# Down projection of a mixture-of-experts kernel in pairs of experts, with the array split into two row halves for what is left

## The chip, the cores and the metric

The kernel runs as one program on one core of a Trainium2 chip. The number that counts is the device time in microseconds (us), median of three runs: 970.37 us for the kernel before (966.24 to 972.15).

## The reference, cut to what matters

One layer: a linear attention with decay over 4096 tokens of width 512, a layer norm, a mixture of experts, a second layer norm. The change is in the experts. Each of 64 experts takes up to 128 tokens, has a hidden width of I = 192 and gives back rows of width 512:

```python
gx = xp[buf_tok]                                   # 64 x 128 x 512
gu = jnp.einsum('ech,ehi->eci', gx, gate_up_proj)  # 512 -> 2 * 192
g, u = jnp.split(gu, 2, axis=-1)
hid = jax.nn.silu(g) * u
eo = jnp.einsum('eci,eih->ech', hid, down_proj) * buf_w[..., None]   # 192 -> 512
routed = jnp.zeros((T + 1, h), x.dtype).at[buf_tok.reshape(-1)].add(eo.reshape(-1, h))[:T]
shared = jax.nn.silu(xf @ shared_gate_w.T) * (xf @ shared_up_w.T) @ shared_down_w.T
return (routed + shared).reshape(b, s, h)
```

All is float32. The reduction of the down projection (`eo`) runs over 192 rows, one and a half times the 128 rows of the TensorE array. The shared expert has a hidden width of 384 and sees all tokens.

## The kernel before

**Stages.** The kernel is written engine by engine, each with its own order written out by hand and semaphores between them. First come 32 attention steps (8 blocks of 512 tokens, 4 chunks each) with routing behind them, then the loop over 64 experts, then a tail that finishes the shared expert and the last layer norm.

**An expert on TensorE (PE).** For expert e the loop issues 12 products of `wgu_hi`, `wgu_lo` with `xgt_hi`, `xgt_lo` into one of `gu_ps` (gate and up), then `turn_rows(e + 1)` (4 transposes of the gathered rows `xg`), then `down(e - 1)`, then the shared units that `fills_of[e]` gives to this expert, then 2 transposes of `hid_e` into `ht_ps`. `down(e)` multiplies the turned hidden rows `hid_et` (two chunks of `IH` = 96 rows) with `wdn` into the one bank `eo_ps`. Both operands are plain float32, and the trace shows each such matmul as two instructions. `down(e)` waits for ScalarE's copy `hid_et` and for ScalarE's emptying of the bank (`eo_done`).

**The other engines.** ScalarE (ACT) copies: `tanh_e`, `xgt_hi` (`split_rows`), `wgu_hi` (`split_expert`), `eo` (`scale_rows`, one of NEO = 3 slots, which waits until the scatter of three experts before has landed, semaphores `rows_added`), then `hid_et`. It works these strictly in that order. GpSimd (POOL) issues `add_rows(e - 2)`, an indirect DMA that adds the 128 rows of `eo` into `acc_rows` in device memory, and `gather(e + 4)`, the rows for an expert four ahead. A scatter waits for the scatter two before it (`rows_added[e % 2]`). SyncE (SP) issues the loads: `wgu` (4 buffers, issued when the product that used the buffer is done) and `wdn` (3 buffers).

**Shared units.** The shared expert is cut into 64 units, 8 for a block of 512 tokens: six products (gate and up of three chunks, 12 matmuls each) and two pairs of output tiles (18 matmuls each). A unit writes one of three banks `proj_ps` (a pair of tiles two), by the rule take % 3, and waits for what emptied the bank three takes before. 8 units run among the last attention steps, 5 ahead of the experts, 21 among the experts, 30 behind them. For the last four blocks (`EARLY` = 4) an output tile is emptied out of its bank by VectorE (DVE) in `add_shared` (`fin_added`), which needs the finished sums of that block in `fin` and `odd`, loaded from `acc_rows`; SP issues these loads only after all 64 scatters have landed:

```python
sp.wait_ge(eo_done, NE)
sp.wait_ge(rows_added[0], 16 * NE // 2)
sp.wait_ge(rows_added[1], 16 * NE // 2)
for m in range(NFA):
    load_first(m)
```

Of the kernel before, what the change touches and what calls it, by code (L numbers as in the profile page):

```python
# [15 lines left out]
P = 128  # L16
# [29 lines left out]
def build(nc, x, x_t, w_qkv, w_out, decay_param, gate_t, w_gu, w_down, sg_t, su_t, sd_t, out):  # L46
# [10 lines left out]
    IH = I // 2  # L57
# [5 lines left out]
    NG, ND, NXG, AHEAD = 4, 3, 6, 4  # L63
    STEPS = NB * KC
    UNITS = 2 * SC + NJ // 2

    assert SC < NJ and KC == NJ and SI == GU and NB % 2 == 0
# [22 lines left out]
    wdn_buf = [both.place(f"wdn{i}", [IH, 2, D]) for i in range(2)]  # L90
# [91 lines left out]
    shared_stage = Map(nc, both.at - 2 * 4 * (KC * GU + 2 * D), both.at)  # L182
# [10 lines left out]
    wdn_buf += [late.place(f"wdn{i}", [IH, 2, D]) for i in range(2, ND)]  # L193
    assert late.at <= projected_end + 8 * 4 * BT

# [11 lines left out]
    hid_et = [late.place(f"hid_et{i}", [IH, 2, P]) for i in range(2)]  # L207
# [7 lines left out]
    fin_map = Map(nc, both.at - 2 * 4 * (KC * GU + 2 * D), both.at)  # L215
# [54 lines left out]
    HEAD = 2  # L270
# [42 lines left out]
    with ExitStack() as ctx:  # L313
# [10 lines left out]
        xg_ps, gu_ps, ht_ps, eo_ps = banks[3], banks[4:6], banks[6], banks[7]  # L324
# [74 lines left out]

        def x1_slot(i):  # L400
            return (NSTAGE + i) % NJ
# [4 lines left out]
        def _(sp):  # L406
# [38 lines left out]
            def load_down(e):  # L445
                if e >= ND:
                    sp.wait_ge(eo_mm, e - ND + 1)
                sp.dma_start(wdn_buf[e % ND][:, :, :], w_down[e]).then_inc(dn_in[e % ND], 16)
# [95 lines left out]
            for e in range(2, ND):  # L544
                load_down(e)
# [16 lines left out]
            for e in range(2):  # L562
                load_down(e)
# [14 lines left out]
            for e in range(NE):  # L578
                if e + NG < NE:
                    load_gate_up(e + NG)  # L580
                if e and e - 1 + ND < NE:
                    load_down(e - 1 + ND)
# [41 lines left out]
        def _(act):  # L624
# [112 lines left out]
            def unit():  # L737
                b, part = divmod(unit_at[0], UNITS)
                unit_at[0] += 1
                if part < 2 * SC:  # L740
                    c = part // 2
                    n = SC * b + c
                    if part % 2 == 0:
                        act.wait_ge(g_mm, n + 1)
                        if n:
                            act.wait_ge(silu_done, n)
                        ps = proj_ps[(unit_take(b) + part) % 3]
# [12 lines left out]
                for j in (2 * pair, 2 * pair + 1) if b < EARLY else ():  # L760
                    act.wait_ge(down_mm, NJ * b + j + 1)
                    if b == 0 and j == 0:
                        act.wait_ge(heads_mm, 2 * NB)
                    if b == 1 and j == 0:
                        act.wait_ge(rest_mm, NT)
                        act.wait_ge(out_mm, NT)
                        act.wait_ge(table_done, TABLE_JOINED)
                    if b >= len(shared_rows) and j == 0:
                        act.wait_ge(shared_out[b - len(shared_rows)], 16)
                    act.copy(shared_rows[b % len(shared_rows)][:, j, :], proj_ps[rows_take[b, j] % 3][:, :]).then_inc(rows_copied, 1)  # L770
# [104 lines left out]
            def scale_rows(e):  # L875
                act.wait_ge(eo_mm, e + 1)
                if e >= NEO:
                    act.wait_ge(rows_added[e % 2], 16 * ((e - NEO) // 2 + 1))
                act.activation(eo[eo_slot[e]][:, :], eo_ps[:, :], ACT.Copy, scale=xg[e % NXG][:, D + e:D + e + 1]).then_inc(eo_done, 1)  # L879
# [19 lines left out]
            for e in range(NE):  # L899
# [8 lines left out]
                if e:  # L908
                    scale_rows(e - 1)
# [5 lines left out]
                act.copy(hid_et[e % 2][:, :, :], ht_ps[0:IH, 0:2 * P].rearrange("p (h s) -> p h s", h=2)).then_inc(hid_et_done, 1)  # L915
# [40 lines left out]
        def _(dve):  # L956
# [232 lines left out]
            def finish_pair(n):  # L1189

                joined = [join_sums(n), join_sums(n + 1)]
                for t in range(2):
                    b, j = fin_order[n + t]
                    dve.wait_ge(down_mm, NJ * b + j + 1)
                    add_shared(n + t, proj_ps[rows_take[b, j] % 3][:, :], joined[t])
# [6 lines left out]
            def unit():  # L1202
                b, part = divmod(unit_at[0], UNITS)
                unit_at[0] += 1
                if part < 2 * SC:
                    c = part // 2
                    n = SC * b + c
                    ps = proj_ps[(unit_take(b) + part) % 3]
# [228 lines left out]
        def _(pool):  # L1437
# [167 lines left out]
        def _(pe):  # L1605
# [5 lines left out]
            def project(s, it, c, n, done):  # L1611
# [3 lines left out]
                if take >= 3:  # L1615
                    pe.wait_ge(*freed[take - 3])
                for k in range(KC):
# [4 lines left out]
                    mm = chain(proj_ps[take % 3][:, :], three(wqkv_hi[:, i, k, :], wqkv_lo[:, i, k, :], x_hi[it % 2][:, k, :],  # L1622
# [112 lines left out]
            def unit():  # L1735
                b, part = divmod(unit_at[0], UNITS)
                unit_at[0] += 1
                if part < 2 * SC:
# [6 lines left out]
                    pe.wait_ge(*freed[take - 3])  # L1745
# [3 lines left out]
                    chain(proj_ps[take % 3][:, :], products).then_inc(u_mm if part % 2 else g_mm, 1)  # L1749
# [3 lines left out]
                for late_chunk in (False, True):  # L1753
                    for j in pair:
# [3 lines left out]
                        if not late_chunk:  # L1758
                            pe.wait_ge(*freed[take - 3])
# [4 lines left out]
                        mm = chain(proj_ps[take % 3][:, :], products, first=not late_chunk, final=late_chunk)  # L1764
# [100 lines left out]
            for e in range(NE):  # L1865
# [10 lines left out]
                if e:  # L1876
                    down(e - 1)
                for _ in range(fills_of[e]):
# [4 lines left out]
                for k in range(2):  # L1883
                    mm = pe.transpose(ht_ps[0:IH, k * P:(k + 1) * P], hid_e[e % 2][:, k * IH:(k + 1) * IH], ident[:, :])
                mm.then_inc(ht_mm, 1)
            down(NE - 1)

# [33 lines left out]
```

## Time and profile before

| what | value |
|---|---|
| median of three runs | 970.37 us (966.24 to 972.15) |
| span of the profiled execution | 967.4 us |
| PE busy | 943.6 us, 98% |
| DVE, ACT, POOL busy | 683.8, 502.8, 466.4 us |
| last 40 us of the expert loop and start of the tail (840 to 880 us) | DMA at 214 GB/s |

The profile gives the execution it shows by its span, from the first to the last instruction; it has no other time for it. The span lies inside the range of the three runs, 3.0 us (0.3%) under their median. The stages in that span: attention to about 410 us, a mixed stretch to about 500 us, the experts to about 863 us, the tail to the end. PE busy is the time in which a matmul record is open, and records overlap, so 98% says that PE has almost always something in hand, not that it is at its peak.

### The profile page before, as it was taken

What the parts mean: (1) busy time and instruction counts of PE and PEld (TensorE: products, weight loads), DVE (VectorE), ACT (ScalarE), POOL (GpSimd) and SP (SyncE); (2) the same over time, 40 slices, a digit from 0 to 9 for tenths busy, and PEclk for the clock granted to TensorE, in tenths of its full rate; (3) what the DMA queues carried; (4) which work ended last, traced back from release to release, by engine and by line L of the source; (5) the groups of instructions that cost most, each with busy time, mean ns of one, the idle gap of its engine ahead of it and who ended that gap; (6) DMA issues with size and microseconds to landing.
All of it is one profiled execution on the core that took longest, in us unless ns stands there. A gap on an engine that the chain in (4) does not pass through costs nothing. (4 is left out here: it accounts for less than half of the span.)

```text
span 967.4 us, 15236 instructions
## 1 busy us (share of the span) xinstructions
PE 943.6 (98%) x4658; PEld 757.0 (78%) x4658; DVE 683.8 (71%) x1251; ACT 502.8 (52%) x1015; POOL 466.4 (48%) x543
## 2 busy tenths in 40 slices
PE   8999999999999999999999999999999999999996
PEld 7888888888888888877887777777767777777875
DVE  7977786969778796887766565566565665636776
ACT  5532434434443443534447665566655665635775
POOL 4002264565556554587234544445545454432564
PEclk9999999999999999989999999999999999999999
DMA  6343452444252434346569999999999999979973
GB/s 202 96 145 109 144 125 91 131 114 132 80 167 91 119 109 140 103 152 231 171 195 272 292 323 307 310 318 294 327 319 316 308 318 298 320 135 372 373 268 118
DMA packets 114191, 203.93 MB, mean 211 GB/s; under 512 B 18496, under 2 KB 56384, under 8 KB 113088
## 3 DMA queue, kind: packets, MB, share of 16 engines
q1 hardware_dynamic: 93584, 159.87, 50.6%
q0 software_dynamic: 19520, 35.75, 16.3%
q10 hardware_dynamic: 1008, 7.34, 2.0%
q8 instruction: 39, 0.64, 0.3%
q14 instruction: 40, 0.33, 0.1%
HBM read 143.03 MB, written 59.88 MB: 210 GB/s over the span
## 5 line engine op out<-in xcount | busy, mean ns | idle before, releaser
L1511 POOL DMA_INDIRECT slot_table<-tokens,slot_of x162 | 179.2, 1106 | 112.0 <-issue 59.6
L1553 POOL DMA_INDIRECT acc_rows<-eo,table_sb x64 | 112.0, 1750 | 170.4 <-ACT eo L879 133.0
L1608 PE MATMUL bank<-x_hi,wqkv_hi 128*128 128x512 f32 x384 | 153.2, 399 | 1.4 <-DVE wqkv_lo L963 1.3
L1376 DVE TENSOR_TENSOR wgu_lo<-wgu,wgu_hi 128x1536 fp32r<-128x1536 f32 x64 | 112.4, 1758 | 55.0 <-ACT wgu_hi L873 55.0
L1608 PE MATMUL bank<-x_hi,wqkv_lo 128*128 128x512 f32 x384 | 150.8, 393 | 0.0
L1608 PE MATMUL bank<-x_lo,wqkv_hi 128*128 128x512 f32 x384 | 150.6, 392 | 0.0
L1608 PE MATMUL bank<-wdn,hid_et 96*128 96x512 f32 x256 | 122.1, 599 | 7.6 <-ACT hid_et L915 7.6
L873 ACT CAST wgu_hi<-wgu 128x1536 fp32r<-128x1536 f32 x64 | 94.5, 1477 | 12.5 <-DMA wgu<-w_gu 12.1
L1542 POOL DMA_INDIRECT xg<-x_rows,table_sb x64 | 74.9, 1170 | 42.0 <-DVE table_sb L1111 22.7
L1608 PE MATMUL bank<-wgu_hi,xgt_hi 128*128 128x384 f32 x256 | 91.6, 358 | 0.0
L647 ACT ACTIVATE e<-bank 128x512 f32<-128x512 f32 x64 | 38.0, 594 | 97.3 <-PE bank L1608 97.3
L1608 PE MATMUL bank<-wgu_hi,xgt_lo 128*128 128x384 f32 x256 | 86.0, 336 | 0.0
L1608 PE MATMUL bank<-wgu_lo,xgt_hi 128*128 128x384 f32 x256 | 85.9, 336 | 0.0
L1608 PEld LDWEIGHTS bank<-x_hi,wqkv_hi 128*128 128x128 f32 x384 | 72.7, 189 | 16.3 <-DVE wqkv_lo L963 2.0
L1608 PEld LDWEIGHTS bank<-x_hi,wqkv_lo 128*128 128x128 f32 x384 | 72.5, 189 | 16.0
L1608 PEld LDWEIGHTS bank<-x_lo,wqkv_hi 128*128 128x128 f32 x384 | 72.6, 189 | 14.8
L1608 PEld LDWEIGHTS bank<-wdn,hid_et 96*128 96x128 f32 x256 | 43.5, 190 | 40.2 <-issue 30.7
L1403 DVE SCALAR_TENSOR_TENSOR silu_e<-tanh_e,bank 128x192 f32<-128x192 f32 x64 | 22.6, 353 | 66.9 <-ACT tanh_e L903 66.7
L1495 POOL TENSOR_SCALAR rstd<-mv 128x1 f32<-128x1 f32 x32 | 9.2, 286 | 115.3 <-DVE mv L990 114.0
L879 ACT ACTIVATE eo<-bank,xg 128x512 f32<-128x512 f32 x64 | 44.3, 692 | 39.2 <-DMA acc_rows<-eo,table_sb 33.9
L1608 PE MATMUL bank<-wout_hi,att_hi 128*128 128x512 f32 x128 | 52.0, 407 | 1.7 <-issue 1.2
L903 ACT ACTIVATE tanh_e<-bank 128x192 f32<-128x192 f32 x64 | 21.2, 331 | 61.6 <-PE bank L1608 61.3
(179 smaller groups left out, 2211.6 us busy)
## 6 DMA issues: line engine op xcount, KB each, us to landing
wgu<-w_gu SPq DMA_DIRECT2D x64, 768.0 KB, 8.8
wdn<-w_down SPq DMA_DIRECT2D x64, 384.0 KB, 8.8
xres<-x SPq DMA_DIRECT2D x32, 256.0 KB, 3.2
x_turned<-x1t SPq DMA_DIRECT2D x32, 256.0 KB, 2.8
x_rows<-x SPq DMA_DIRECT2D x32, 256.0 KB, 3.1
acc_rows<-x SPq DMA_DIRECT2D x32, 256.0 KB, 3.1
fin<-acc_rows SPq DMA_DIRECT2D x8, 1024.0 KB, 12.1
odd<-acc_rows SPq DMA_DIRECT2D x8, 1024.0 KB, 13.5
```

The source lines that it names most:

```text
L647: act.activation(e_sb[q][:, :], ps[:, :], ACT.Exp)
L873: act.copy(wgu_hi[e % 2][:, :, :], wgu_buf[e % NG][:, :, :]).then_inc(wgu_hi_done, 1)
L879: act.activation(eo[eo_slot[e]][:, :], eo_ps[:, :], ACT.Copy, scale=xg[e % NXG][:, D + e:D + e + 1]).then_inc(eo_done, 1)
L903: act.activation(tanh_e[:, :], gu_ps[e % 2][:, 0:I], ACT.Tanh, scale=0.5).then_inc(tanh_e_done, 1)
L1376: dve.tensor_tensor(wgu_lo[e % NG][:, :, :], wgu_buf[e % NG][:, :, :], wgu_hi[e % 2][:, :, :].bitcast(F32), ALU.subtract).then_inc(wgu_lo_ ...
L1403: dve.scalar_tensor_tensor(out=silu_e[:, :], in0=tanh_e[:, :], scalar=1.0, in1=ps[:, 0:I], op0=ALU.add, op1=ALU.mult).then_inc(silu_e_done, 1)
L1495: pool.tensor_scalar(rstd[i][:, :], mv[i][:, 1:2], EPS_NORM, None, ALU.add).then_inc(norm_done, 1)
L1511: pool.indirect_dma_start(table_dram, bass.IndirectOffsetOnAxis(slot_of[:, i, k:k + 1], 0), tokens[:, i:i + 1], None, bounds_check=SLOTS - ...
L1542: pool.indirect_dma_start(xg[e % NXG][:, :], None, x1_dram, bass.IndirectOffsetOnAxis(table_sb[:, e:e + 1], 0), bounds_check=T - 1, oob_is ...
L1553: pool.indirect_dma_start(acc_dram[e % 2], bass.IndirectOffsetOnAxis(table_sb[:, e:e + 1], 0), eo[eo_slot[e]][:, :], None, bounds_check=T ...
L1608: mm = pe.matmul(out_ap, a, b, start=first and i == 0, stop=final and i == len(products) - 1)
```

## The change

`down` no longer takes 192 rows as 96 + 96. For a pair of experts (even e and odd e) the weights come as one tile of three planes of 128 rows: 128 rows of the even expert, 128 rows of the odd one, and a plane that holds the 64 rows left of the even expert in rows 0 to 63 and the 64 left of the odd one in rows 64 to 127. `down(e)` is now one matmul over 128 rows; behind the odd one, `down_rest(p)` issues four matmuls of 64 rows and 256 columns, alternately in the upper and the lower row half, into two banks. Bank 2 is lent by the shared units for this while the expert loop lasts (they use banks 0 and 1 then). ScalarE scales both experts of a pair behind each other, in the iteration after the pair. `HEAD` goes from 2 to 6, so that 25 shared units (21 before) run among the experts and 26 (30 before) behind them, and units stand at odd experts alone. The weight loads are half as many and twice as large, with 2 buffers of a pair instead of 3 of an expert.

```diff
-    NG, ND, NXG, AHEAD = 4, 3, 6, 4
+    NG, ND, NXG, AHEAD = 4, 2, 6, 4
...
-    hid_et = [late.place(f"hid_et{i}", [IH, 2, P]) for i in range(2)]
+    hid_et = [late.place(f"hid_et{i}", [P, 2, P]) for i in range(2)]
...
-    HEAD = 2
+    HEAD = 6
...
-        while done < total and (done - first_units) * NE < (e + 1) * (total - first_units):
+        while e % 2 and done < total and (done - first_units) * NE < (e + 1) * (total - first_units):
...
-        xg_ps, gu_ps, ht_ps, eo_ps = banks[3], banks[4:6], banks[6], banks[7]
+        xg_ps, gu_ps, ht_ps, eo_ps = banks[3], banks[4:6], banks[6], [banks[7], banks[2]]
...
+        for take in range(3 * STEPS, len(freed)):
+            lent = first_units <= unit_of(take) < total
+            if lent and not eo_lent:
+                eo_emptied, eo_lent = freed[last_in[2]], True
+            bank = min((0, 1) if lent else (0, 1, 2), key=lambda n: last_in[n])
+            bank_of.append(bank)
+            if bank == 2 and eo_lent:
+                emptied.append((eo_done, NE))
+                eo_lent = False
...
+            def load_down(p):
+                if p >= ND:
+                    sp.wait_ge(eo_mm, 2 * (p - ND + 1))
+                sp.dma_start(wdn_buf[p % ND][:, :, :], w_down[p]).then_inc(dn_in[p % ND], 16)
...
-                if e:
+                if e and e % 2 == 0:
+                    scale_rows(e - 2)
                     scale_rows(e - 1)
...
-            for e in range(NE):
-                if e >= 2:
-                    add_rows(e - 2)
-                if e + AHEAD < NE:
-                    gather(e + AHEAD)
+            for e in range(0, NE, 2):
+                for n in (e, e + 1):
+                    if e:
+                        add_rows(n - 2)
+                    if n + AHEAD < NE:
+                        gather(n + AHEAD)
...
             def down(e):
+                p, r = divmod(e, 2)
                 pe.wait_ge(hid_et_done, e + 1)
-                pe.wait_ge(dn_in[e % ND], 16 * (e // ND + 1))
-                if e:
-                    pe.wait_ge(eo_done, e)
-                chain(eo_ps[:, :], [(hid_et[e % 2][:, k, :], wdn_buf[e % ND][:, k, :]) for k in range(2)]).then_inc(eo_mm, 1)
+                pe.wait_ge(dn_in[p % ND], 16 * (p // ND + 1))
+                if p:
+                    pe.wait_ge(eo_done, e - 1)
+                elif r:
+                    pe.wait_ge(*eo_emptied)
+                pe.matmul(eo_ps[r][:, :], hid_et[r][:, 1 - r, :], wdn_buf[p % ND][:, r, :], start=True, stop=False)
+
+            def down_rest(p):
+
+                for half in range(2):
+                    cols = slice(half * D // 2, (half + 1) * D // 2)
+                    for r in range(2):
+                        rows = slice(r * REM, (r + 1) * REM)
+                        mm = pe.matmul(eo_ps[r][:, cols], hid_et[r][rows, r, :], wdn_buf[p % ND][rows, 2, cols], start=False, stop=half == 1)
+                        if half:
+                            mm.then_inc(eo_mm, 1)
```

The order of PE in the middle of the loop, before: two experts without a shared unit between them, the products `wgu` left out.

```order
L1844 MATMUL bank3<-ident_49,xg3_184 128x128 [waits xgt_lo_done,xg_in3]
L1608 MATMUL bank7<-wdn1_73,hid_et1_197 128x512 [waits eo_done,dn_in1,hid_et_done]
L1608 MATMUL bank7<-wdn1_73,hid_et1_197 128x512
L1884 MATMUL bank6<-ident_49,hid_e0_194 96x128 [waits hid_et_done,hid_e_done]
...
L1844 MATMUL bank3<-ident_49,xg4_200 128x128 [waits xgt_lo_done,xg_in4]
L1608 MATMUL bank7<-wdn2_177,hid_et0_196 128x512 [waits eo_done,dn_in2,hid_et_done]
```

The same place of PE in the changed kernel: a pair, with a shared unit of output tiles (`sd`) in its odd iteration.

```order
L1879 MATMUL bank7<-wdn0_72,hid_et0_195 128x512 [waits eo_done,dn_in0,hid_et_done]
L1632 MATMUL bank1<-sd_hi_165,hid_hi_159 128x512 [waits hid_lo_done,rows_copied,shared_split]
...
L1868 MATMUL bank3<-ident_49,xg3_183 128x128 [waits xgt_lo_done,xg_in3]
L1879 MATMUL bank2<-wdn0_72,hid_et1_196 128x512 [waits eo_done,dn_in0,hid_et_done]
L1887 MATMUL bank7<-wdn0_72,hid_et0_195 128x256
L1887 MATMUL bank2<-wdn0_72,hid_et1_196 128x256
L1887 MATMUL bank7<-wdn0_72,hid_et0_195 128x256
L1887 MATMUL bank2<-wdn0_72,hid_et1_196 128x256
L1923 MATMUL bank6<-ident_49,hid_e0_193 128x128 [waits hid_et_done,hid_e_done]
```

Of each expert's two matmuls one is gone, and four of half the columns stand behind the odd expert's, before the next transposes.

ScalarE before, in two iterations of the loop: one `eo` in each, ahead of `hid_et`.

```order
L879 ACTIVATE eo1_190<-bank7,xg4_200 128x512 [waits rows_added0,eo_mm]
L915 COPY hid_et1_197<-bank6 96x256 [waits eo_mm,ht_mm]
L903 ACTIVATE tanh_e_192<-bank4 128x192 [waits silu_e_done,gu_mm]
L867 CAST xgt_hi1_186<-bank3 128x512 [waits gu_mm,xgt_mm]
L873 CAST wgu_hi0_198<-wgu0_70 128x1536 [waits gu_mm,gu_in0]
L879 ACTIVATE eo2_191<-bank7,xg5_201 128x512 [waits rows_added1,eo_mm]
```

ScalarE in the changed kernel, the same stretch: none in the odd iteration, two in the even one.

```order
L937 COPY hid_et1_196<-bank6 128x256 [waits eo_mm,ht_mm]
L924 ACTIVATE tanh_e_191<-bank4 128x192 [waits silu_e_done,gu_mm]
L888 CAST xgt_hi1_185<-bank3 128x512 [waits gu_mm,xgt_mm]
L894 CAST wgu_hi0_197<-wgu0_70 128x1536 [waits gu_mm,gu_in0]
L900 ACTIVATE eo2_190<-bank7,xg2_182 128x512 [waits rows_added0,eo_mm]
L900 ACTIVATE eo0_188<-bank2,xg3_183 128x512 [waits rows_added1,eo_mm]
L937 COPY hid_et0_195<-bank6 128x256 [waits eo_mm,ht_mm]
```

Two waits for a scatter now stand right behind each other ahead of one `hid_et`.

PE at the start of the tail, before: behind the last `wdn` come four units of products, the first of which is shown.

```order
L1608 MATMUL bank7<-wdn0_72,hid_et1_197 128x512
L1608 MATMUL bank0<-x1t_hi_165,sg_hi_159 128x512 [waits rows_copied,x1t_lo_done,shared_split]
```

PE at the start of the tail, changed: behind the last piece come at once the output tiles, the fourth of which waits for `fin_added`.

```order
L1887 MATMUL bank2<-wdn1_176,hid_et1_196 128x256
L1632 MATMUL bank2<-sd_hi_165,hid_hi_159 128x512 [waits hid_lo_done,eo_done,shared_split]
...
L1632 MATMUL bank0<-sd_hi_165,hid_hi_159 128x512 [waits hid_lo_done,hid_s_done,shared_split]
...
L1632 MATMUL bank2<-sd_hi_165,hid_hi_159 128x512 [waits hid_lo_done,fin_added]
```

The four units that stood ahead of this wait now run in the loop.

## Rows read from the trace of the kernel before

**Rows 1.** The page: busy times, granted TensorE clock and DMA share in 40 slices

```profile
PE 943.6 (98%) x4658; PEld 757.0 (78%) x4658; DVE 683.8 (71%) x1251; ACT 502.8 (52%) x1015; POOL 466.4 (48%) x543
...
PEclk9999999999999999989999999999999999999999
DMA  6343452444252434346569999999999999979973
```

**Rows 2.** Stretches: length, PE, PEld, DVE, ACT, POOL busy, granted clock, DMA share, GB/s

```profile
520.00:840.00 320.00, 313.21 (x1493) 241.33 (x1492) 192.54 (x255) 196.52 (x317) 162.32 (x112) 0.99 1.04 311
560.00:600.00 40.00, 39.03 (x186) 29.46 (x185) 24.62 (x34) 24.37 (x39) 18.40 (x13) 1.00 1.05 314
680.00:720.00 40.00, 40.00 (x194) 30.53 (x193) 25.31 (x35) 25.70 (x41) 24.39 (x16) 1.00 1.05 326
722.00:724.00 2.00, 0.30 (x3) 0.06 (x1) 0.00 (x0) 0.56 (x1) 0.00 (x0) 1.00 1.05 297
724.00:726.00 2.00, 1.57 (x3) 0.68 (x4) 1.31 (x3) 2.00 (x5) 0.21 (x1) 0.90 1.06 323
726.00:728.00 2.00, 2.00 (x5) 1.25 (x4) 1.52 (x1) 1.14 (x2) 1.69 (x2) 0.50 1.04 311
728.00:730.00 2.00, 2.00 (x8) 1.54 (x8) 0.24 (x1) 0.00 (x0) 1.69 (x2) 0.75 1.03 310
880.00:960.00 80.00, 78.21 (x337) 62.52 (x336) 61.11 (x128) 57.24 (x114) 43.80 (x116) 1.00 0.77 283
```

**Rows 3.** Timeline of PE in the loop: start, length, instruction, count

```profile
701.02 0.60 PE L1844 MATMUL bank<-ident,xg 128*128 128x128 f32 x4
701.45 1.88 PE L1608 MATMUL bank<-wdn,hid_et 96*128 96x512 f32 x4
703.17 0.38 PE L1884 MATMUL bank<-ident,hid_e 128*96 128x128 f32 x2
703.31 0.42 PE L1608 MATMUL bank<-wgu_hi,xgt_hi 128*128 128x384 f32 x1
703.57 0.33 PE L1608 MATMUL bank<-wgu_lo,xgt_hi 128*128 128x384 f32 x1
...
705.50 0.60 PE L1844 MATMUL bank<-ident,xg 128*128 128x128 f32 x4
...
712.72 0.49 PE L1844 MATMUL bank<-ident,xg 128*128 128x128 f32 x3
```

**Rows 4.** Durations of one form, min/median/max ns, 520 to 850 us

```profile
L1608 PE MATMUL bank<-wdn,hid_et x228: 591/592/1061, 525.9 to 844.4; 96*128 96x512 f32 x114
```

**Rows 5.** Who waited for whom, 520 to 862 us: total, times, longest us

```profile
ACT eo L879 <- DMA acc_rows<-eo,table_sb: 33.9, 17, 3.8
...
ACT wgu_hi L873 <- DMA wgu<-w_gu: 12.1, 11, 2.3
...
PE bank L1608 <- ACT hid_et L915: 7.6, 7, 2.1
```

**Rows 6.** The scatters of 520 to 862 us, from issue to landing

```profile
DMA to landing us min/median/max: 4.8/9.7/12.4
```

**Rows 7.** DMA issues of 560 to 600 us, median us to landing

```profile
wgu<-w_gu SPq DMA_DIRECT2D x7, 768.0 KB, 13.7
```

**Rows 8.** DMA issues of 680 to 720 us, median us to landing

```profile
wgu<-w_gu SPq DMA_DIRECT2D x8, 768.0 KB, 8.6
```

**Rows 9.** Timeline of all engines, from the last expert to the tail

```profile
861.81 1.98 PE L1608 MATMUL bank<-wdn,hid_et 96*128 96x512 f32 x4 [0.81 <-ACT hid_et L915]
...
863.84 0.69 ACT L879 ACTIVATE eo<-bank,xg 128x512 f32<-128x512 f32 x1 [2.07 <-PE bank L1608]
...
865.28 1.55 POOL L1553 DMA_INDIRECT acc_rows<-eo,table_sb  x1 [1.47 <-ACT eo L879]
...
870.22 0.39 SPq L589 DMA_DIRECT2D fin<-acc_rows  x1
...
880.75 0.50 PE L1608 MATMUL bank<-sd_hi,hid_hi 128*128 128x512 f32 x1 [0.61 <-DVE fin L1170]
```

More of the change, by code:

```diff
@@ L56, in build @@
     SC = SI // P
-    IH = I // 2
+    REM = I - P
     SLOTS = E * CAP
@@ L89, in build @@
     wgu_buf = [both.place(f"wgu{i}", [P, KC, GU]) for i in range(2)]
-    wdn_buf = [both.place(f"wdn{i}", [IH, 2, D]) for i in range(2)]
+    wdn_buf = [both.place("wdn0", [P, 3, D])]
     att = Map(nc, both.at, end)
@@ L192, in build @@
     wgu_lo = [Map(nc, at, at + 4 * KC * GU).place(f"wgu_lo{i}", [P, KC, GU], F32R) for i, at in enumerate(wgu_at)]
-    wdn_buf += [late.place(f"wdn{i}", [IH, 2, D]) for i in range(2, ND)]
     assert late.at <= projected_end + 8 * 4 * BT
+    wdn_buf += [late.place(f"wdn{i}", [P, 3, D]) for i in range(1, ND)]
     shared_rows = [late.place(f"shared_rows{b}", [P, NJ, D]) for b in range(EARLY - SET)]
@@ L398, in unit_take, with unit_of @@
             return 3 * STEPS + b * (2 * SC + NJ)
+        def unit_of(take):
+            b, n = divmod(take - 3 * STEPS, 2 * SC + NJ)
+            return b * UNITS + (n if n < 2 * SC else 2 * SC + (n - 2 * SC) // 2)
+        bank_of = [take % 3 for take in range(3 * STEPS)]
+        emptied = [freed[take - 3] if take >= 3 else None for take in range(3 * STEPS)]
+        last_in = {bank: 3 * STEPS - 3 + bank for bank in range(3)}
+        eo_emptied, eo_lent = None, False
+        for take in range(3 * STEPS, len(freed)):
[7 more added lines that the diff above has]
+                eo_lent = False
+            else:
+                emptied.append(freed[last_in[bank]])
+            last_in[bank] = take
         def x1_slot(i):
@@ L1615, in project @@
                 if take >= 3:
-                    pe.wait_ge(*freed[take - 3])
+                    pe.wait_ge(*emptied[take])
                 for k in range(KC):
@@ L1744, in unit @@
                     pe.wait_ge(x1t_lo_done, KC * (b + 1))
-                    pe.wait_ge(*freed[take - 3])
+                    pe.wait_ge(*emptied[take])
                     products = []
@@ L1748, in unit @@
                         products += three(w_hi[:, k, cols], w_lo[:, k, cols], x1t_hi[:, k, :], x1t_lo[:, k, :])
-                    chain(proj_ps[take % 3][:, :], products).then_inc(u_mm if part % 2 else g_mm, 1)
+                    chain(proj_ps[bank_of[take]][:, :], products).then_inc(u_mm if part % 2 else g_mm, 1)
                     return
@@ L1758, in unit @@
                         if not late_chunk:
-                            pe.wait_ge(*freed[take - 3])
+                            pe.wait_ge(*emptied[take])
                         pe.wait_ge(hid_lo_done, SC * b + (SC if late_chunk else SC - 1))
@@ L1763, in unit @@
                             products += three(hid_hi[:, c, tok], hid_lo[:, c, tok], sd_hi[:, c, :], sd_lo[:, c, :])
-                        mm = chain(proj_ps[take % 3][:, :], products, first=not late_chunk, final=late_chunk)
+                        mm = chain(proj_ps[bank_of[take]][:, :], products, first=not late_chunk, final=late_chunk)
                         if late_chunk:
@@ L1877, in _ @@
                     down(e - 1)
+                if e and e % 2 == 0:
+                    down_rest(e // 2 - 1)
                 for _ in range(fills_of[e]):
@@ L1902 @@
     gu, down = a["L0_ffn_gate_up_proj"], a["L0_ffn_down_proj"]
-    experts, inner = gu.shape[0], down.shape[1] // 2
+    experts, rest = gu.shape[0], down.shape[1] - P
     gu = gu.reshape(experts, D // P, P, -1).transpose(0, 2, 1, 3)
-    down = down.reshape(experts, 2, inner, D).transpose(0, 2, 1, 3)
+    even, odd = down[0::2], down[1::2]
+    shared_chunk = np.concatenate([even[:, :rest], odd[:, P:]], axis=1)
+    down = np.stack([even[:, rest:], odd[:, :P], shared_chunk], axis=2)
     decay = np.repeat(a["L0_attn_decay_param"], D // HEADS).reshape(D // P, P).T
```

38 lines of the change are left out of this document (18 added, 20 removed).

## The prediction

> **What bounds the kernel now.** I read the page first. PE has a record open 98% of the span, the granted clock stands at 9 tenths or more in all slices, and the DMA engines, a third to a half busy in attention, stand at 9 through the expert loop [rows 1]. So two resources are full at once in the loop, and the question is which of them a cheaper down projection meets next. Among the stretches the reader should look at the last two columns: from 520 to 840 us the share is 1.04 at 311 GB/s. Where PE never idles (680 to 720 us) DMA moves 326 GB/s, the highest of these stretches, and weights land in 8.6 us; at 560 to 600 us it gives 314, and the weights need 13.7 us [rows 2, 7, 8]. DMA is thus hardly below what it can give: 326 / 311 is 4.8%, and of the 343 us from 520 us to the last expert at 863.5 us at most 16 us could be taken before DMA stops it. Who waits: PE stands idle only for ScalarE's `hid_et`, 7.6 us in 7 waits. ScalarE itself waits 33.9 us for scatters to land and 12.1 us for weights [rows 5]. The longest of PE's waits lies at 722 to 724 us, and behind it the granted clock is 0.50: PE works at 1.2 instead of 2.4 GHz for a while. Over the three rows from 724 to 730 us the missing clock is 2 x 0.10 + 2 x 0.50 + 2 x 0.25 = 1.7 us of work [rows 2]. In the tail PE is busy 78.2 of 80 us [rows 2]: from the first finished tile to the end PE's order sets the time. The tail's start is a chain I come to below [rows 9].
>
> **What the change does to PE's work in the loop.** Four instructions of `wdn` take 701.45 to 703.17 us, 1.72 us, 0.43 for 512 columns [rows 3]. A pair costs 3.44 now. After: two whole matmuls, four instructions, 1.72; and four pieces of 256 columns, eight instructions of 0.215. How far the pieces of the two row halves run together no row shows. Serial, they take 1.72 and nothing is saved. Perfectly together they take 0.86, and 32 x 0.86 = 27.5 us is saved. I take the case between: instructions start in order, and the two of one matmul use the same half, so the second waits for the first. Then the slots are A1, A2+B1, B2+C1, C2+D1, D2: five of 0.215, 1.07 us. A pair costs 2.79, saves 0.65, and 32 pairs save 20.8 us.
>
> The array goes over from whole to halves and back once per pair, 64 changes. No row has it. Where the form changes now (96 rows to 128, float32 to the split products) nothing is lost: from 703.17 us two transposes of 0.108 (0.43 for four) and one product of 0.17 end at 703.56, and the next product starts at 703.57 [rows 3]. That is the low end, 0. The high end is a pipeline run empty: the record of a `wdn` matmul is 592 ns long where its successor starts after 430, so 0.16 us [rows 4], 10.4 us in all. I take 0.05, nearer to the row of a change of form: 3.2 us.
>
> The four units: the distance of two `xg` transposes is 4.48 us without a unit and 7.22 with one [rows 3], so a unit of products is 2.74 us, 0.228 per matmul, and four put 11.0 us into the loop. PE's work in the loop changes by -20.8 + 3.2 + 11.0 = -6.6 us. The transposes of `hid_e` with 128 columns for 96 stream the same identity, ScalarE's copy is of 256 columns as before on more partitions: nothing. Weight loads carry the same bytes; halving their number and doubling their size changes how far ahead they are issued, by some 3 us of 17, and they stay ahead of the 8.6 to 13.7 us that loads need now: nothing, unless landing grows.
>
> **What it does to the waits in the loop.** Half of the `eo` of a pair must now follow the other at once. `eo` of the odd expert needs the slot whose scatter is the even one of the pair before, issued one pair ago instead of three experts ago. The ring is: `eo` 0.69 us, issue 0.75 us after its end (864.53 to 865.28), landing 9.7 us, less the 0.6 by which the second `eo` follows the first: 10.5 us [rows 6, 9]. A pair with a unit of products costs PE 2 x 4.48 - 0.65 + 0.10 + 2.74 = 11.15 us, more than the ring; the 7 of 32 pairs that have no unit cost 8.4. There ScalarE waits about 2.1 us. Queued behind it are `hid_et`, `tanh_e`, `xgt_hi` and `wgu_hi`; PE needs `hid_et` 2.6 us after the transposes (703.31 to 705.94), ScalarE's two `eo` and the copy fill some 2.0 of these, so 0.6 is slack and 1.5 reaches PE: 7 x 1.5 = 10 us of idle, in place of 7.6 now. Loop: -6.6 + 2.4 = -4.2 us. That asks DMA for 311 x 343 / 339 = 315 GB/s, which it has given.
>
> **What it does to the tail.** Now the last `wdn` ends at 861.81 + 4 x 0.43 = 863.5 us. From there: `eo` 863.84, scatter 865.28, loads of `fin` 870.22, first bank emptied 880.75 [rows 9], that is 17.2 us. PE covers it: four units 11.0, one pair of tiles 18 x 0.228 = 4.1, the first six matmuls of the next 1.4, and 0.6 of idle is left. After, the four units are gone from here, while the chain hangs on the last scatter and doesn't move with them. It gets longer: both `eo` of the last pair stand behind the last piece, and POOL must issue two scatters behind each other (0.3 + 0.69 + 0.75 for the first, 1.55 busy and some 0.3 for the second): 3.6 us to the second against 1.8 now, +1.9 us. PE has 1.6 us to wait for the lent bank, works 5.5, and then idles about 12 us. So the four units gain nothing here: they are paid in the loop and the time they leave is a wait. And 12 us of idle is followed by half clock as at 724 us: +1.7 us [rows 2]. Tail: +3.6 us from the last expert to the end. Sum: -4.2 + 3.6 = -0.6 us. Against the span of 967.4 us that is 966.8; the median stands 3.0 us above this span, so 969.8, and I say **970 us**. A measurement of this kernel can tell about 1%, 9.7 us, from no change.
>
> **A rule against the change.** What stands here is needed by nothing else. The Trainium skill, TensorEngine Tiling (Array Packing), section Key Properties, says that a change of the tiling mode drains TensorE. In this trace no row shows one; if it holds, the high end of 0.16 us is the price, and that rival follows. The same skill, TensorE: Matmul & The Clock Gate, Part 3, gives 3.07 times for four row tiles and says that matmuls start and end in program order; by the order alone the sum is the five slots I took.
>
> **The rivals.**
> *Every change of mode empties the array* (0.12). 64 x 0.16 = 10.4 in place of 3.2: 977 us. For it: the 162 ns by which a record outlasts its successor's start. Against: no change of form costs anything now.
> *The halves don't run together: the change doesn't do what it says* (0.19). Plain float32 matmuls are two instructions each, and no row shows two at once. Nothing saved: loop +11.0 + 0 to 3.2, less about half of today's 7.6 us of idle, which a slower PE doesn't meet, tail +3.6: +11 to +14, 981 to 984 us, with full drains 991.
> *The ring of scatters decides: slower* (0.15). Place: the second `eo` of each even iteration. Two scatters and two gathers now go out in one burst, so a landing may take more than 9.7 us; today's longest is 12.4. It decides from about 10.9 us, where more than the unitless pairs begin to wait. At 11.0 us the ring is 11.8: 7 x 2.8 = 20 us of idle, +8 to 9 in all, 979. At 11.4 us it is 12.2: 7 x 3.2 + 25 x 0.5 = 35 us, 994. Centre 984. For it: ScalarE waits 33.9 us for scatters already, with three experts' distance, and the longest stall of PE came so.
> *DMA follows and PE takes all: faster* (0.10). -20.8 + 11.0 - 7.6 (no idle left) = -17, cut by DMA to -16, tail +3.6: -12, 958 us. For it: 326 GB/s in one stretch. Against: it needs the best stretch through the whole loop.
>
> **How the numbers follow.** The forecast, 0.44, spans 962 to 977 (pieces 0.86 to 1.07 us, changes 0 to 0.08, idle 5 to 14 us). The likeliest gives the time, 970. From 961 to 986 us lie the forecast, the drain, most of the two slower rivals; left out are most of the faster one and the far ends of the ring, 0.15 to 0.2. Faster by over 1% is the faster rival, 0.10; slower by over 1% is the serial one with four fifths of the ring, 0.32; the rest, 0.58, is within 1%.
>
> **What would show it.** The pieces: from the last whole `wdn` matmul's end to the next transposes about 1.1 us, 1.7 or more if serial, 0.16 more on either side if the array drains. The loop: last down near 859 us, DMA share still above 1 at 311 to 318 GB/s. The waits: ScalarE's `eo` for `acc_rows` in pairs without a unit, PE's idle for `hid_et` near 10 us. The tail: one PE wait of about 12 us on `fin_added`, some 7 us behind the last piece, half clock after it, and then the same 79 us of PE work. Wrong I would be if DMA gave more than 326 GB/s with the larger loads, if landings passed 11 us, or if the first bank were emptied much sooner than 10.5 us after `fin` is issued (870.22 to 880.75).

## The result and the profile after

The changed kernel takes 1004.05 us (median of 4, 1002.52 to 1004.97), beside 969.71 us for the kernel before (median of 4, 966.24 to 972.15): 1.036 of its time, interval 1.033 to 1.040, 34 us slower. The prediction said 970, at most 986.

The page of the changed kernel: busy times, then the granted clock and the DMA share in 40 slices, and its last part, the median us from issue to landing. It answers to [rows 1].

```profile
PE 941.0 (94%) x4786; PEld 759.3 (76%) x4786; DVE 684.9 (68%) x1251; ACT 503.7 (50%) x1015; POOL 485.5 (48%) x543
...
PEclk9999999999999999989999999899989999997999
DMA  6333525334343316276569999899989899859963
...
wgu<-w_gu SPq DMA_DIRECT2D x64, 768.0 KB, 6.6
wdn<-w_down SPq DMA_DIRECT2D x32, 768.0 KB, 6.2
```

PE has a record open for 2.6 us less than before, in a span that is 35.7 us longer: it waits. In the slices of the expert loop the clock shows two eights, before only nines, and the DMA share is four times eight (the five is the slice in which the loop ends, where before has a seven). Weights land after 6.2 to 6.6 us; on the page of before it is 8.8 for both. So neither PE's work nor DMA can be what got longer.

A window over the loop, beside the first of [rows 2], for the changed kernel (length, busy times of PE, PEld, DVE, ACT and POOL, granted clock, DMA share, GB/s):

```profile
520.00:880.00 360.00, 329.33 (x1696) 258.11 (x1695) 202.56 (x267) 204.60 (x329) 188.31 (x115) 0.96 0.94 286
```

PE idles 360 - 329.33 = 30.7 us; before it is 320 - 313.21 = 6.8 in 320 us. The mean clock of 0.96 is 0.04 x 360 = 14.4 us of missing clock, before 0.01 x 320 = 3.2; these two are rounded to 0.01, and the ledger below has them finer.

Who waited for whom, changed kernel, 520 to 895 us (total, times, longest), beside [rows 5]:

```profile
ACT eo L900 <- DMA acc_rows<-eo,table_sb: 42.0, 11, 7.3
...
PE bank L1879 <- ACT hid_et L937: 27.4, 10, 4.5
```

Before, ScalarE waited 17 times for a scatter, at most 3.8 us; now 11 times, up to 7.3 us, and nearly all of PE's idle is the wait for `hid_et` behind it. The scatters themselves, over the same window, do not land later in the median than before (9.7 us, [rows 6]), but sooner:

```profile
DMA to landing us min/median/max: 4.7/7.8/12.1
```

The longest of these waits, first on GpSimd, then ScalarE, then PE (start, length, engine and line; in brackets the idle time ahead and what ended it):

```profile
726.61 1.81 POOL L1576 DMA_INDIRECT acc_rows<-eo,table_sb  x1 [3.09 <-ACT eo L900]
...
730.08 1.59 POOL L1576 DMA_INDIRECT acc_rows<-eo,table_sb  x1 [0.30 <-issue]
...
737.87 1.59 POOL L1576 DMA_INDIRECT acc_rows<-eo,table_sb  x1 [4.85 <-DMA acc_rows<-eo,table_sb]
...
725.13 1.28 ACT L900 ACTIVATE eo<-bank,xg 128x512 f32<-128x512 f32 x2
...
734.18 0.69 ACT L900 ACTIVATE eo<-bank,xg 128x512 f32<-128x512 f32 x1
742.15 0.69 ACT L900 ACTIVATE eo<-bank,xg 128x512 f32<-128x512 f32 x1 [7.28 <-DMA acc_rows<-eo,table_sb]
742.74 0.36 ACT L937 COPY hid_et<-bank 128x256 f32<-128x256 f32 x1
...
738.99 0.93 PE L1868 MATMUL bank<-ident,xg 128*128 128x128 f32 x4 [2.35 <-DMA xg<-x_rows,table_sb]
743.15 2.08 PE L1879 MATMUL bank<-wdn,hid_et 128*128 128x512 f32 x2 [3.24 <-ACT hid_et L937]
```

The pair's two scatters go out 3.5 us apart, since a gather lies between them on GpSimd. The second `eo` of the next pair, ready at 734.9, starts at 742.15, 12.1 us after the issue of the *second* scatter at 730.08. The first, of 726.61, had landed by 737.87 at the latest: GpSimd then issued the next scatter of its parity, which waits for it. If `eo` had waited for that one, it would have started over 4 us sooner. PE idles twice here, 2.35 us for gathered rows and 3.24 for `hid_et`.

That is the code, read again. `scale_rows(e)` writes the slot `eo[e % 3]`, but waits for `rows_added[e % 2]`, the semaphore of its own parity, to reach 16 x ((e - 3) // 2 + 1). For odd e that count is reached with the scatter of expert e - 2, for even e with that of expert e - 4, and an even e leans on the wait of the odd one ahead of it. The section on the kernel before says that `eo` waits for the scatter of three experts before, and my prediction reckoned so; that is true of the slot, not of the wait. An odd e asks for a newer scatter than its slot needs. With one scatter per iteration the two are an iteration apart; with pairs it is the second scatter of the pair before, the newest of all.

**Where the deep waits lie.** Six of ScalarE's 11 waits are longer than 5 us (5.2 to 7.3) and make 34 of the 42 us. Five of the six lie in pairs without a shared unit: there the first `eo` of two pairs start 9.0 to 9.2 us apart (725.13 and 734.18 above), with a unit some 11.2. The second scatter ahead of the six took 9.9 to 12.1 us to land. Behind the other second scatters, 4.7 to 9.6 us, ScalarE waited 2.8 us at most. So the damage is not spread over all pairs.

### The profile page after: what moved, and what is told of

It is laid out like the page before. It is cut to its first block and busy times, and to the rows that moved or that the text cites. A ratio compares the mean times of both kernels' runs of the same rounds, so it can differ in the third digit from the quotient of the medians.

```text
span 1003.1 us, 15460 instructions
## 1 busy us (share of the span) xinstructions
PE 941.0 (94%) x4786; PEld 759.3 (76%) x4786; DVE 684.9 (68%) x1251; ACT 503.7 (50%) x1015; POOL 485.5 (48%) x543
## 5 line engine op out<-in xcount | busy, mean ns | idle before, releaser
L1576 POOL DMA_INDIRECT acc_rows<-eo,table_sb x64 | 127.5, 1992 | 183.7 <-ACT eo L900 163.1
L1565 POOL DMA_INDIRECT xg<-x_rows,table_sb x64 | 79.9, 1248 | 42.0 <-DVE table_sb L1134 22.7
L1879 PE MATMUL bank<-wdn,hid_et 128*128 128x512 f32 x128 | 70.5, 634 | 27.4 <-ACT hid_et L937 27.4
L900 ACT ACTIVATE eo<-bank,xg 128x512 f32<-128x512 f32 x64 | 42.1, 687 | 46.7 <-DMA acc_rows<-eo,table_sb 43.0
L1632 PE MATMUL bank<-sd_hi,hid_hi 128*128 128x512 f32 x96 | 42.6, 444 | 14.3 <-DVE fin L1193 11.0
```

What stands on the lines that cost most here:

```text
L900: act.activation(eo[eo_slot[e]][:, :], eo_ps[e % 2][:, :], ACT.Copy, scale=xg[e % NXG][:, D + e:D + e + 1]).then_inc(eo_done, 1)
L1565: pool.indirect_dma_start(xg[e % NXG][:, :], None, x1_dram, bass.IndirectOffsetOnAxis(table_sb[:, e:e + 1], 0), bounds_check=T - 1, oob_is ...
L1576: pool.indirect_dma_start(acc_dram[e % 2], bass.IndirectOffsetOnAxis(table_sb[:, e:e + 1], 0), eo[eo_slot[e]][:, :], None, bounds_check=T ...
L1632: mm = pe.matmul(out_ap, a, b, start=first and i == 0, stop=final and i == len(products) - 1)
L1879: pe.matmul(eo_ps[r][:, :], hid_et[r][:, 1 - r, :], wdn_buf[p % ND][:, r, :], start=True, stop=False)
```

## The experiments

Times are medians, each with the ratio to the kernel before on the same chip and its interval. "Loop end" is the end of the last product with `wdn` in the profiled execution; it was 863.5 us before and is 894.8 in the changed kernel.

**Which scatter does `eo` wait for?** In the changed kernel one index is altered, so that `eo` waits for exactly the scatter that used its slot:

```diff
-                    act.wait_ge(rows_added[e % 2], 16 * ((e - NEO) // 2 + 1))
+                    act.wait_ge(rows_added[(e - NEO) % 2], 16 * ((e - NEO) // 2 + 1))
```

> The changed kernel with one index altered: an eo copy waits for the scatter of three experts before (whose slot it takes), not for the newest scatter of its own parity, which for an odd expert is the one of two experts before. Theory ring (the second eo of a pair waits for the second scatter of the pair before, which GpSimd issues some 5 us after the first): the ring gets some 3 to 4 us shorter, ScalarE's 42 us of waiting for scatters falls below 20, PE's idle for hid_et from 27 us below 12; time 975 to 985 us. Rival order (PE idles because hid_et stands behind two eo, wherever the scatters are): nothing changes, 1000 to 1006. Rival DMA (the larger weight loads lower what DMA gives): 1000 to 1006.

Measured: 965.44 us, 0.997 (0.995 to 1.000), 39 us under the changed kernel (38 by the two ratios), and some 10 us under the lower end of what was expected. Windows and waits of this run:

```profile
520.00:840.00 320.00, 311.58 (x1661) 246.08 (x1660) 199.00 (x262) 200.19 (x321) 174.84 (x114) 1.00 1.00 316
```

```profile
PE bank L1868 <- DMA xg<-x_rows,table_sb: 7.1, 6, 2.1
...
ACT eo L900 <- DMA acc_rows<-eo,table_sb: 5.4, 5, 1.6
...
PE bank L1879 <- ACT hid_et L937: 0.5, 1, 0.5
```

ScalarE's wait falls from 42.0 to 5.4 us, PE's for `hid_et` from 27.4 to 0.5, the clock is whole again, and the loop ends at 860.2. The index by itself carries the whole loss.

**The same from other sides.** A fourth slot with the exact index (`eo` of three slots gets one more), and, with the old wait and three slots, one `eo` per iteration again:

```diff
-                if e and e % 2 == 0:
-                    scale_rows(e - 2)
-                    scale_rows(e - 1)
+                if e >= 2:
+                    scale_rows(e - 2)
```

> The changed kernel with four eo slots in place of three, and the wait for exactly the scatter that freed the slot. Theory ring: two pairs of scatters may be in flight on ScalarE's side, its wait for scatters nearly vanishes (below 8 us); what is left is GpSimd's own wait for the scatter of two before. Time 970 to 980 us. Rivals order and DMA: 1000 to 1006.

> The changed kernel with one eo copy in each iteration (expert e - 2 in iteration e) in place of two in the even ones; three slots and the old wait. Theory ring: the scatters are a burst no longer, the distance between an odd scatter and the next odd eo is again two iterations less the issue, as in the kernel before; time 972 to 985. Rival order: the same gain, so this run alone doesn't tell the two apart, a_slot does. Rival DMA: 1000 to 1006.

Four slots: 965.80 us, 0.998 (0.996 to 1.001), loop end 856.5. In the profiled executions the loop ends 3.7 us sooner than with three, but the medians don't differ (the profiled execution of `a_slot` took 969.89 us, 4 more than its median). One `eo` per iteration: 969.48 us, 1.002 (0.999 to 1.004), ScalarE's wait for scatters 6.3 us in 8. Both gained more than expected. Either the strict wait or the bunching of the two `eo` had to go, and one was enough: the loss needs both.

**The strict wait in the kernel before.** If ScalarE's 33.9 us of waiting for scatters [rows 5] held the loop up there too, the exact index alone would gain.

> The kernel before with the same index altered in the wait of the eo copies. Theory ring: the 7.6 us of PE's idle for hid_et in its loop and ScalarE's 34 us for scatters come from the same wait; both fall, and 3 to 9 us are gained, 961 to 967. Rival DMA (the loop of the kernel before is at DMA's limit): within 2 us of 970, with weights landing later in place of it.

Measured: 970.55 us, 1.003 (1.000 to 1.007): nothing gained. Waits, the page's weight loads and the window of this run:

```profile
ACT wgu_hi L873 <- DMA wgu<-w_gu: 53.6, 34, 3.2
...
PE bank L1608 <- ACT hid_et L915: 3.9, 5, 1.1
PE bank L1608 <- DMA wdn<-w_down: 3.9, 3, 1.6
```

```profile
wgu<-w_gu SPq DMA_DIRECT2D x56, 768.0 KB, 13.1
```

```profile
520.00:840.00 320.00, 313.17 (x1496) 240.69 (x1495) 189.99 (x255) 195.72 (x316) 163.27 (x112) 1.00 1.05 311
```

ScalarE's wait for scatters is replaced by one for weights, 53.6 us in 34 waits (12.1 before), which land after 13.1 us (9.6 in the same window of before), at a share of 1.05 (1.04 before) and the same 311 GB/s. PE waits 3.9 us for `hid_et` and 3.9 for `wdn`, where it waited 7.6 for `hid_et`: its idle stays as it was. Before, the loop had DMA as its second limit, and a wait taken off one engine only moved to the next.

**The four units.** `HEAD` back to 2 in the changed kernel (`a_head2`), in the one with four slots and exact index (`a_four_head2`), and 6 instead of 2 in the kernel before (`b_head6`):

> The changed kernel with HEAD = 2: the four shared units (11.0 us of PE) go back out of the expert loop to the tail; three eo slots and the old wait stay. Theory ring (the loop of the changed kernel is set by eo, scatter, landing, eo and not by PE): the loop is not shortened by the 11 us that PE no longer does in it, PE's idle grows by as much; the tail covers its chain again, which saves the 1.7 us of half clock: 1000 to 1004. Rival (PE's work and its order set the loop): 990 to 994.

> Four eo slots and HEAD = 2. Where the ring is gone, theory PE: the loop gets 11 us shorter and the tail, whose first bank is emptied 19 us after the last piece whatever PE does, keeps its length less 1.7 us of half clock: 953 to 957. Theory DMA (the loop stands at what DMA gives, 320 GB/s in a_four): the loop shortens by at most 3 to 7 us, weights land later than 10 us, ScalarE waits for them: 957 to 963.

> The kernel before with HEAD = 6: the four units move into the loop and nothing else. My account of the tail: they are paid in the loop (11.0 us, less up to 4 us of idle that a slower PE doesn't meet) and leave a wait of about 12 us on the first emptied bank, with 1.7 us of half clock behind: 976 to 981. Rival (moving work from the tail to a loop that is DMA's is free, and the tail gets 11 us shorter): 958 to 962.

Waits of `a_head2`, 520 to 850 us:

```profile
ACT eo L900 <- DMA acc_rows<-eo,table_sb: 47.5, 11, 5.9
...
PE bank L1879 <- ACT hid_et L937: 31.9, 10, 4.7
```

With four units fewer this kernel is *slower*: 1013.66 us, 1.048 (1.045 to 1.051), loop end 899.1, past what I had expected. Up to its loop end ScalarE waits 50.0 us in 12 waits and PE 33.7 us in 12 (42.0 in 11 and 27.4 in 10 with the units). 11 pairs are without a unit (7 with `HEAD` 6), and such pairs are where the deep waits lie. The 11.0 us of work taken out of the loop come back as idle (38.0 us from 520 us to the loop end, 31.5 with the units) and as half clock (18.8 us of missing clock against 13.6). These make the loop 0.7 us longer; it is 4.3 us longer, and the rest is not accounted for, nor why the medians are 9.6 us apart where the profiled executions differ by 3.0.

With the ring gone the same edit gains: 958.55 us, 0.991 (0.989 to 0.993), against 965.80 with `HEAD` 6. That is in the range I gave to a limit by DMA, but its sign is missing: ScalarE doesn't wait for weights, which land after 7.5 to 8.2 us. And the units alone, in the kernel before, cost: 974.48 us, 1.007 (1.003 to 1.010), a little under what was expected, with this in its tail:

```profile
888.37 0.80 PE L1608 MATMUL bank<-sd_hi,hid_hi 128*128 128x512 f32 x1 [11.23 <-DVE fin L1170]
```

The idle of 11 us in front of the first tile of the tail that the prediction reasoned out of the order is there, without pairs too.

**How the pieces run.** Three variants, all with four slots and the exact index. In `a_four_serial` the four pieces go upper, upper, lower, lower instead of alternately; in `same_half` all use rows 0 to 63 (the odd expert's last 64 rows are then those of other data, and its output with them); in `full_cols` there are two pieces of 512 columns:

```diff
-                        rows = slice(r * REM, (r + 1) * REM)
+                        rows = slice(0, REM)
```

> Four eo slots, and the four pieces in the order upper, upper, lower, lower instead of alternately. Slot theory (instructions start in order, the two of one matmul and all of one half follow each other, only different halves overlap): seven slots of 0.215 us instead of five, 1.5 us from the first piece to the next transposes instead of 1.06; the loop some 10 to 14 us longer, less what idle takes up. Rival (the two halves don't really overlap, the 64-row pieces are shorter for another reason): 1.06 us again.

> Four eo slots, and all four pieces take rows 0 to 63, so the pieces of the odd expert multiply other rows than the reference's (its result is another by that; count and sizes of instructions are the same). If the time of the pieces comes from two different row halves working at once, the same half has to take them one after another: 8 x 0.215 = 1.7 us to the next transposes. If 64-row pieces are short for another reason: 1.06 us again.

> Four eo slots, and the pieces as two matmuls of 64 rows and 512 columns, one in each half, instead of four of 256. Slot theory of the prediction (in order, the second instruction of a matmul waits for the first): three slots of 0.43, 1.3 us. If PE pairs instructions of the two halves whatever their order, as the order upper, upper, lower, lower hinted: two slots, 0.95 to 1.06 us. If the halves don't overlap: 1.7 us.

A piece group and the transposes behind it, in the changed kernel, then in the three in that order. The distance of the two starts is what the group costs PE:

```profile
711.85 1.02 PE L1879 MATMUL bank<-wdn,hid_et 128*128 128x512 f32 x2
712.80 1.14 PE L1887 MATMUL bank<-wdn,hid_et 64*128 64x256 f32 x8
713.87 0.44 PE L1923 MATMUL bank<-ident,hid_e 128*128 128x128 f32 x2
714.06 0.42 PE L1632 MATMUL bank<-wgu_hi,xgt_hi 128*128 128x384 f32 x1
```

```profile
706.06 1.14 PE L1888 MATMUL bank<-wdn,hid_et 64*128 64x256 f32 x8
707.13 0.44 PE L1924 MATMUL bank<-ident,hid_e 128*128 128x128 f32 x2
```

```profile
706.86 1.99 PE L1888 MATMUL bank<-wdn,hid_et 64*128 64x256 f32 x8
708.78 0.44 PE L1924 MATMUL bank<-ident,hid_e 128*128 128x128 f32 x2
```

```profile
707.75 1.13 PE L1886 MATMUL bank<-wdn,hid_et 64*128 64x512 f32 x4
708.81 0.44 PE L1920 MATMUL bank<-ident,hid_e 128*128 128x128 f32 x2
```

1.07, 1.07, 1.92 and 1.06 us; the three variants took 965.78, 990.06 and 969.69 us (one time each). The order of the pieces doesn't matter, their number and width don't, and one half alone takes 1.92. The overlap is real and comes from the different halves. Streaming is 8 x 0.215 = 1.72 us; 1.92 is 0.20 more, and 1.72 / 2 + 0.20 = 1.06. These sums fit halves that overlap wholly, at 0.20 us of fixed cost, and not the five slots that I had: in the order upper, upper, lower, lower the slots would have been seven, 1.5 us. How PE pairs pieces in that order the records don't tell, since they don't name the half. That `same_half` costs 24 us, while 0.85 x 32 is 27, also shows how nearly each us of PE's loop work counts once the ring is gone.

**The order on GpSimd, the strict wait kept.** Both scatters ahead of both gathers, so that the second scatter goes out right behind the first:

```diff
                 for n in (e, e + 1):
                     if e:
                         add_rows(n - 2)
+                for n in (e, e + 1):
                     if n + AHEAD < NE:
                         gather(n + AHEAD)
```

> The changed kernel (three slots, old wait) with GpSimd's order in a pair as scatter, scatter, gather, gather. Theory ring: the second scatter is issued 1.4 us earlier, and the ring of a pair shrinks by that, from about 12.2 to 10.9 us, below PE's 11.2 for most pairs; two thirds or more of the loss goes: 975 to 988 us. If burst and contention on DMA, not the issue of the second scatter, set the landing: no change, 1000 to 1006.

```profile
PE bank L1869 <- DMA xg<-x_rows,table_sb: 20.8, 7, 4.5
...
ACT eo L900 <- DMA acc_rows<-eo,table_sb: 17.5, 6, 4.6
...
PE bank L1880 <- ACT hid_et L937: 0.5, 1, 0.5
```

990.68 us, 1.023 (1.019 to 1.026), 13 us under the changed kernel, and less than the two thirds of the loss that were expected. The waits are those of 520 to 881 us, the loop end of this run. ScalarE's wait for the scatter shrinks from 42.0 to 17.5 us, and PE's for `hid_et` from 27.4 to 0.5. Gathers, now issued later, take its place: PE waits 20.8 us for `xg` (2.6 in the changed kernel). With the second scatter right behind the first the ring hardly reaches PE by way of `hid_et`, as the timeline has it; what is left of the loss comes by way of the gathers.

**A version that beats both.** The waits of `a_four_head2` name what is next:

```profile
POOL acc_rows L1577 <- DMA acc_rows<-eo,table_sb: 40.0, 17, 4.0
...
PE bank L1869 <- DMA xg<-x_rows,table_sb: 8.0, 9, 2.1
```

GpSimd waits for the scatter two before, and the gather queued behind that wait comes late for PE. So: six slots and the exact index as above, `HEAD` 2, and each gather ahead of its scatter.

```diff
-    HEAD = 6
+    HEAD = 2
...
                 for n in (e, e + 1):
-                    if e:
-                        add_rows(n - 2)
                     if n + AHEAD < NE:
                         gather(n + AHEAD)
+                    if e:
+                        add_rows(n - 2)
```

> Six eo slots, HEAD = 2 and on GpSimd the gather of each expert ahead of its scatter, so that no gather stands behind a scatter that waits for the one of two before. With four slots and HEAD = 2 PE idled 8 us for gathered rows. If the gathers were late by GpSimd's order: that idle goes and 952 to 957 us are reached. If the loop is at DMA's limit of 320 GB/s: idle moves to another wait (weights), 957 to 961.

```profile
520.00:840.00 320.00, 317.99 (x1706) 251.02 (x1705) 205.10 (x269) 208.88 (x335) 188.40 (x118) 1.00 1.01 324
```

```profile
863.97 0.50 PE L1633 MATMUL bank<-sd_hi,hid_hi 128*128 128x512 f32 x1 [1.17 <-DVE fin L1194]
```

952.39 us, 0.983 (0.981 to 0.986). PE idles 2.0 us in 320, DMA moves 324 GB/s, the loop ends at 844.7, and the tail's wait is 1.17 us. This is what was expected if the gathers were late by GpSimd's order. The slots and the order were changed together, so the runs don't part the two. The kernel before was not run with six slots and the gather first, so how much of the 15 us belongs to the pairs stays open.

## Why the prediction was wrong, point by point

**The step that failed** is the first of the part on the waits: "`eo` of the odd expert needs the slot whose scatter is the even one of the pair before". By the code it waits for the odd one. My ring was 0.69 + 0.75 + 9.7 - 0.6 = 10.5 us. With the second scatter in it, 3.5 us later, it is 0.69 + 0.75 + 3.5 - 0.6 = 4.34 us and the landing. Against pairs without a unit, which take 9.0 to 9.2 us (8.4 in my sum), this gives the deep waits nearly to the digit: with landings of 9.9, 10.5 and 12.0 us it is 5.2, 5.7 and 7.3 us, where 5.2, 5.65 and 7.28 were measured, and not my 2.1. With a unit, 11.2 us, a landing of 9.6 gives 2.7, measured 2.8, and the median of 7.8 gives 0.9. So the place was right, the pairs without a unit, and the length of the wait was wrong; at worst it reaches pairs with a unit too (12.1 us of landing, a wait of 5.3). The slack of 0.6 us that I gave PE was 1.2: a wait of ScalarE of 5.33 us reached PE as 4.13.

**The loop's ledger**, +31.3 us at its end. Idle from 520 us to the loop end: 31.5 against 7.6, +23.9. Half clock behind the idle, the missing clock of the same stretch added up in steps of 2 us: 13.6 against 1.7, +11.9. PE's work: 3.44 us per pair became 1.71 for the whole matmuls, 0.10 ahead of the pieces (711.85 to 712.80 is 0.95, and two instructions stream for 0.86), 1.06 for them, and 0.05 behind (the transposes to the next product 0.19, [rows 3] 0.14), 2.92. That saves 0.52, times 32 is 16.6; less the 11.0 of the four units, -5.6. The sum is +30.2; of the 1.1 us left over, 1.0 is idle from 480 to 520 us (1.2 against 0.2). I had put the idle at 10 us and left the clock out of the loop's sum, though [rows 2] showed both at 722 to 730 us: a third of the damage is PE working at 1.2 GHz after it had stood. By these two sums each us that PE stood in the loop cost about half a us more. That is no rule: `a_slot` and `b_slot` idle 9.2 and 8.7 us in their loops, at most 2.1 us at once, and their clock misses nothing.

**The rival of the ring** had the right place, the second `eo` of each even iteration, and a wrong condition: a landing above 10.9 us. Landings got shorter in the median, 7.8 us, and the ring decided all the same. Its time of 984 was 20 us short, its far end of 994 still 10. I had costed the wait from the slot and not from the semaphore and the count beside it, which stand in a line that the change leaves alone.

**What was right.** The pieces: 1.07 us predicted, 1.07 measured, by luck, since the composition was wrong. The change of mode: 0.10 us per pair predicted, 0.15 measured outside the pieces, 1.6 us more in all. Serial halves are out, and so is the time of the rival in which every change empties the array, which put 0.32 us on top of the five slots. What it supposes is not out: with the 0.20 inside, a pair pays 0.35 us beyond its streaming, and two changes at 0.16 would be 0.32. No run parts a cost of the change from another fixed cost of the group. With the index put right the sum itself holds: `a_slot` ends its loop at 860.2 us (predicted 859.3) and has a span of 968.0 (predicted 966.8). By the medians it is 2.8 us under the kernel before, where the sum had 0.6. One slip in the chances: the serial rival with four fifths of the ring is 0.31, not 0.32.

**The tail** went as it was worked out. PE in the changed kernel, from the last piece on:

```profile
893.75 1.13 PE L1887 MATMUL bank<-wdn,hid_et 64*128 64x256 f32 x8
...
897.40 0.47 PE L1632 MATMUL bank<-sd_hi,hid_hi 128*128 128x512 f32 x1 [2.51 <-issue]
...
913.94 0.79 PE L1632 MATMUL bank<-sd_hi,hid_hi 128*128 128x512 f32 x1 [10.82 <-DVE fin L1193]
```

```profile
913.00:915.00 2.00, 1.06 (x3) 0.87 (x4) 2.00 (x6) 0.74 (x2) 0.68 (x2) 0.50 1.04 383
...
917.00:919.00 2.00, 2.00 (x6) 1.52 (x5) 1.81 (x4) 0.00 (x0) 0.03 (x1) 0.50 1.04 394
```

From the last piece (894.8) to the first tile behind the sums (913.9) are 19.1 us; 17.2 + 1.9 = 19.1 were predicted. The idle was to be 1.6 + 12 us and is 2.5 + 10.8; half clock follows from 913.9 to 920.2 us and costs some 3 us, where I had 1.7. From loop end to span end are 108.3 us, before 103.9: +4.4 for the predicted +3.6. The four units were paid in the loop and saved nothing in the tail, as predicted, and `b_head6` and `a_four_head2` show it from both sides: 6.4 us lost by adding them, 7.2 us gained by leaving them out.

**DMA as the limit** was read rightly for the kernel before (`b_slot`), but 326 GB/s is not the most that the loop gets with the larger loads, one of the signs that I had named for being wrong. `best_gather`, at about the same share, moved more in several stretches of 40 us:

```profile
560.00:600.00 40.00, 39.60 (x216) 30.95 (x212) 26.45 (x35) 26.12 (x43) 24.11 (x15) 1.00 1.04 356
...
680.00:720.00 40.00, 39.80 (x214) 31.31 (x214) 25.70 (x35) 25.01 (x40) 26.30 (x16) 1.00 1.04 346
```

Over 320 us no run moved more than 324. What the ceiling is, and whether the size of the loads moves it, stays open; the failed step doesn't hang on it.

## What to carry to other kernels

When a change bunches work that came evenly, write down every wait of that work as the code has it: the semaphore, the count, and which instruction brings it there. A wait that asks for more than the buffer needs cost nothing here until the change issued two in a row (`b_slot`); then one index was worth 39 us. Judge a resource only with the waits around it right: four units among the experts were a help of 10 us in the one kernel and a loss of 7 us in the other.

## What I had not expected of the hardware

- Pieces in the two row halves overlap in either order of issue, 1.07 us against 1.92 in one half alone. A group costs some 0.20 us beyond its streaming, with 0.10 us ahead of it and 0.05 behind: 0.35 us for a visit to the halves.
- Scatters landed sooner in bursts of two (7.8 us median) than one by one in the kernel before (9.7 us), where DMA moved 311 GB/s and not 286. What slowed the ring was the queue on GpSimd, 3.5 us between the two issues; the longest landing, 12.1 us, is no longer than before's 12.4. Why the second scatters ahead of the deep waits took 9.9 us and more, no run shows.
- Gathers share that queue: putting them behind both scatters took 24.5 us off ScalarE's wait for scatters and put 18.2 us on PE's for gathered rows.
- The same idle can cost clock or not. 31.5 us in stalls of up to 4.5 us went with 13.6 us of missing clock, 9.2 us in stalls of up to 2.1 us (`a_slot`) with none, and in the kernel before one of about 2.1 us with 1.7.
